# A GRU and an attention layer on one core: PSUM banks of two gates laid out by step instead of by sequence

## The reference

```python
def cell(h, x):
    gi = x @ W_ih + b_ih
    gh = h @ W_hh + b_hh
    i_r, i_z, i_n = jnp.split(gi, 3, axis=-1)
    h_r, h_z, h_n = jnp.split(gh, 3, axis=-1)
    r = jax.nn.sigmoid(i_r + h_r)
    z = jax.nn.sigmoid(i_z + h_z)
    n = jnp.tanh(i_n + r * h_n)
    h_new = (1.0 - z) * n + z * h
    return (h_new, h_new)
```

## Time and profile before

| | us |
|---|---|
| median of 3 runs | 746.58 (746.04 to 747.35) |
| the profiled execution | 746.35 |
| its span, first to last instruction | 744.5 |
| TensorE busy | 711.3 (96%) |
| VectorE busy | 580.8 (78%) |
| ACT busy | 484.9 (65%) |
| granted clock, mean | 0.996 |

### The profile page before, as it was taken

How to read it: one execution, slowest core, us unless ns; L and a number is a source line. 1 busy time by engine, 2 the same in 40 slices (tenths; PEclk the granted TensorE clock), 3 DMA queues, 4 the chain that set the end, 5 groups by cost and what they waited for, 6 DMA issues and landing times.

```text
span 744.5 us, 25735 instructions
## 1 busy us (share of the span) xinstructions
PE 711.3 (96%) x10644; PEld 525.3 (71%) x10644; DVE 580.8 (78%) x1625; ACT 484.9 (65%) x1665; POOL 104.4 (14%) x134
## 2 busy tenths in 40 slices
PE   6789999999999989999999999999999999999997
PEld 5688888888888767767667677676666767644555
DVE  5778888888888877777788888788887888834643
ACT  4455666556555666767787777776778776675453
POOL 0232222322322200000000101010110101000040
PEclk9999999999999999999999999999999999999999
DMA  6311121111211012222322222222232233300001
GB/s 237 100 48 46 47 83 51 46 45 46 88 38 40 3 30 43 44 37 49 46 44 44 43 45 44 43 44 49 40 50 43 45 52 37 47 19 29 29 6 52
DMA packets 77869, 36.74 MB, mean 49 GB/s; under 512 B 70540, under 2 KB 73784, under 8 KB 77752
## 3 DMA queue, kind: packets, MB, share of 16 engines
q1 hardware_dynamic: 77175, 33.52, 20.4%
q10 hardware_dynamic: 576, 1.57, 0.6%
HBM read 16.20 MB, written 2.10 MB: 25 GB/s over the span
## 4 chain that ended last, share of the span: by engine, by line
PE 83%; DVE 6%; ACT 4%; DMA 3%; issue 2%; SPq 1%; POOL 0%; DVEq 0%; POOLq 0%
PE bank L429 21%; PE bank L431 20%; PE bank L430 20%; PE bank L536 12%; PE bank L544 5%; DVE h_hi L1211 3%; DMA pT_lo<-p_lo 3%; PE bank L449 2%; ACT zg L937 2%; DVE nu L1205 1%; SPq L308 1%; PE bank L436 1%; DMA x<-in_x 1%; PE bank L458 0%; PE bank L478 0%
## 5 line engine op out<-in xcount | busy, mean ns | idle before, releaser
L431 PE MATMUL bank<-y_lo,w_hi 128*128 128x512 f16 (+2 forms) x496 | 139.8, 300 | 0.0
L429 PE MATMUL bank<-y_hi,w_hi 128*128 128x512 f16 (+2 forms) x496 | 139.7, 300 | 0.1
L430 PE MATMUL bank<-y_hi,w_lo 128*128 128x512 f16 (+2 forms) x496 | 139.8, 300 | 0.0
L536 PE MATMUL bank<-h_hi,whh_hi 128*128 128x16 f16 x1536 | 111.1, 177 | 17.6 <-DVE h_hi L1211 15.2
L536 PEld LDWEIGHTS bank<-h_hi,whh_hi 128*128 128x128 f16 x1536 | 88.8, 96 | 36.7 <-DVE h_hi L1211 34.1
L536 PE MATMUL bank<-h_hi,whh_lo 128*128 128x16 f16 x1536 | 109.5, 176 | 0.4 <-issue 0.4
L997 ACT ACTIVATE prob<-bank,nmx 128x128 f32<-128x128 f32 x256 | 90.4, 366 | 29.8 <-DVE nmx L1286 29.8
L536 PEld LDWEIGHTS bank<-h_hi,whh_lo 128*128 128x128 f16 x1536 | 89.4, 96 | 0.6 <-issue 0.5
L429 PE MATMUL bank<-w_hi,y_hi 128*128 128x128 f16 x512 | 89.1, 219 | 0.5 <-DVE v_lo L1290 0.5
L431 PE MATMUL bank<-w_lo,y_hi 128*128 128x128 f16 x512 | 89.1, 219 | 0.0
L430 PE MATMUL bank<-w_hi,y_lo 128*128 128x128 f16 x512 | 89.1, 219 | 0.0
(11 more groups left out here) (156 smaller groups left out, 2132.9 us busy)
## 6 DMA issues: line engine op xcount, KB each, us to landing
stage<-in_weights SPq DMA_DIRECT2D x16, 640.0 KB, 4.1
x<-in_x SPq DMA_DIRECT2D x16, 128.0 KB, 4.0
out<-xr SPq DMA_DIRECT2D x3, 512.0 KB, 3.1
xr<-in_ada_r SPq DMA_DIRECT2D x1, 1024.0 KB, 7.4
pT_hi<-p_hi SPq DMA_TRANSPOSE x64, 2.4
pT_lo<-p_lo SPq DMA_TRANSPOSE x64, 2.5
xr<-in_W_ih ACTq DMA_DIRECT2D x2, 384.0 KB, 3.9
xr<-in_W_hh ACTq DMA_DIRECT2D x2, 384.0 KB, 5.2
```

The source lines that it names most:

```text
L429: mm(ps, w[0], a[0], start=start, stop=False, skip_group_check=True)
L430: mm(ps, w[1], a[0], start=False, stop=False, skip_group_check=True)
L431: return mm(ps, w[0], a[1], start=False, stop=stop, skip_group_check=True)
L536: nc.tensor.matmul(out(m0 + m), half[:, k, (m0 + m) * P:(m0 + m + 1) * P], h_hi[:, k * B:(k + 1) * B, 1], start=False, stop=False, skip_gr ...
```

## The change

The banks of r and z are laid out by step: the word of `j` and `t` lies at `32 * t + j`. One step's 32 words are adjacent. The input products of m = 0 to 3 write in the order (step, sequence), 16 adjacent words for each step, and read their moving operand in that order as well. The operand stays where it was, so two words that are read one after the other lie 8 fp16 words (16 bytes) apart. `x_bias` writes 32 words of `pick`, eight times over, for r and z. The banks of n, their products and all counts of instructions stay.

```diff
-        r_cols, z_cols = ([ps[:, 0:BS * GB].rearrange("p (j t) -> p j t", t=BS) for ps in pair]
+        r_cols, z_cols = ([ps[:, 0:BS * GB].rearrange("p (t j) -> p t j", t=BS) for ps in pair]
...
-                for ps, at, width in ((r_bank, 0, GB), (z_bank, GB, GB), (n_bank, 2 * GB, 2 * GB)):
-                    nc.tensor.matmul(ps[n % 2][:, 0:BS * width], gpair[:, :],
-                                     pick[:, at:at + width].unsqueeze(2).broadcast_to([GK, width, BS]), start=True,
+                for ps, at in ((r_bank, 0), (z_bank, GB)):
+                    nc.tensor.matmul(ps[n % 2][:, 0:BS * GB], gpair[:, :],
+                                     pick[:, at:at + GB].unsqueeze(1).broadcast_to([GK, BS, GB]), start=True,
                                      stop=False, skip_group_check=True)
+                nc.tensor.matmul(n_bank[n % 2][:, :], gpair[:, :],
+                                 pick[:, 2 * GB:4 * GB].unsqueeze(2).broadcast_to([GK, 2 * GB, BS]), start=True,
+                                 stop=False, skip_group_check=True)
...
-                return (r_cols[n % 2][:, c, :], z_cols[n % 2][:, c, :], n_cols[n % 2][:, c, 1, :])[m // 2]
+                return (r_cols[n % 2][:, :, c], z_cols[n % 2][:, :, c], n_cols[n % 2][:, c, 1, :])[m // 2]
...
-                    nc.tensor.matmul(gate_cols(n, m), w[:, k, m * P:(m + 1) * P], a[:, n % 2, k, :], start=False,
+                    moving = a[:, n % 2, k, :]
+                    if m < 4:
+                        moving = moving.rearrange("p (b t) -> p t b", b=B)
+                    nc.tensor.matmul(gate_cols(n, m), w[:, k, m * P:(m + 1) * P], moving, start=False,
                                      stop=False, skip_group_check=True)
...
-                    return (r_cols[r % 2][:, c, s], z_cols[r % 2][:, c, s], n_cols[r % 2][:, c, 0, s])[m // 2]
+                    return (r_cols[r % 2][:, s, c], z_cols[r % 2][:, s, c], n_cols[r % 2][:, c, 0, s])[m // 2]
...
-                    nc.scalar.activation(zr[:, :, 1], r_cols[r % 2][:, :, s], ACT.Sigmoid).then_inc(r_ok, 1)
+                    nc.scalar.activation(zr[:, :, 1], r_cols[r % 2][:, s, :], ACT.Sigmoid).then_inc(r_ok, 1)
```

More of the change, by code:

```diff
@@ L934, in _ @@
                     act.wait_ge(r_mm, t1)
-                    nc.scalar.activation(zr[:, :, 1], r_cols[r % 2][:, :, s], ACT.Sigmoid).then_inc(r_ok, 1)
+                    nc.scalar.activation(zr[:, :, 1], r_cols[r % 2][:, s, :], ACT.Sigmoid).then_inc(r_ok, 1)
                     act.wait_ge(z_mm, t1)
-                    nc.scalar.activation(zg[:, :], z_cols[r % 2][:, :, s], ACT.Sigmoid).then_inc(z_ok, 1)
-                    nc.scalar.activation(zz[:, :, 1], z_cols[r % 2][:, :, s], ACT.Sigmoid, scale=-1.0)
+                    nc.scalar.activation(zg[:, :], z_cols[r % 2][:, s, :], ACT.Sigmoid).then_inc(z_ok, 1)
+                    nc.scalar.activation(zz[:, :, 1], z_cols[r % 2][:, s, :], ACT.Sigmoid, scale=-1.0)
                     act.wait_ge(npre_ok, t1)
```

## The result

The changed kernel takes 820.0 us (median of 4 runs, 818.2 to 820.3) against 746.8 us for the kernel before. The ratio is 1.0976, interval 1.0957 to 1.0995. The direction was forecast. The size was not: 73 us more instead of 11.8, beyond the range and beyond the dearer rival's 800 us.

A forecast was written before the change was run, and what follows sets the result against it. TensorE, nearly always busy, alternated in the recurrence with turns through ACT and VectorE; slower reads added 11.2 us in 13 blocks, 0.35 and 0.28 around blocks 0 and 1: 11.8 on 746.35, 758.2 us, range 745 to 792.

The forecast's parts named there:

- the dearer rival: Input products of m = 0 to 3 cost VectorE's far-read price, 177 to 229 ns each: 781 to 800 us; 24 in 100.
- The read's price: Input products of m = 0 to 3 on TensorE, read 16 bytes apart: 0.111 us each instead of 0.056.
- the prediction's own signs of being wrong: Cadence staying at 0.055 us or exceeding 0.15, first products' 0.105 us growing, or plain steps changing their 1.91 us.
- the smallest whole step above free: One extra access per word in the distant read, twice the old cadence: 0.111 us a product.
- The upper end: Price from VectorE's `rows_sum`, 256-byte steps: 1.38 to 1.79 ns a word, 177 to 229 ns a product.
- Rooms, counts and shares: Slow products behind s = 1 to 4: 7, 2, 13, 2; room for them: none, 0.21, 0.26, 0.09 us.
- a rule with two halves: Each access crossing to a new 16-byte line pays, yet 8 two-byte words may be strode over for free.
- The start-up: First 36 input products before the first step, already 0.105 us each: nothing charged; 2.5 us if 24 doubled.
- The writes: Input products of m = 0 to 3 writing rows of 16 adjacent words: nothing charged, as n products' runs of 8.
- ACT's reads and `x_bias`: Adjacent gate reads and bias matmuls: gain taken as 0, at most 0.3 and 0.8 us in all.
- The faster rival: Free read, and z products' last writes arrive 0 to 25 ns earlier each step: 744 us; 8 in 100.
- What makes up for it: Nothing after a late step recovers the time; the attention stage shifts whole, its length unchanged.

The follow-up runs named there:

- four adjacent products: Kernel before, with each input product of m = 0 to 3 issued four times, every one reading and writing adjacent words: 799.4 us.
- experiments 1: Kernel before with its old banks; only the moving operand of the products of m = 0 to 3 is read 16 bytes apart: 812.8 us, ratio 1.088.
- 3: Changed kernel's banks, with xb_hi and xb_lo laid out by step so every input product reads adjacent words; n products write 64 bytes apart: 747.7 us, ratio 1.0011.
- after: The changed kernel itself, against the kernel before: 820.0 us, ratio 1.0976.
- 2: Changed kernel's banks, but products of m = 0 to 3 read adjacent words and write each word 128 bytes from the last: 763.2 us, ratio 1.0217.
- spread: Changed kernel with its input products reordered, two slow then one fast, and shared evenly over the steps: 801.2 us.
- the candidate: New banks against the kernel before, a second load of x ordered by step for the conversions, and new shares of input products: 751.0 us, ratio 1.0095.
- experiment 5: Kernel before with its old banks and adjacent reads; products of m = 0 to 3 write each word 8 bytes from the last: 759.1 us.

## Why the prediction was wrong

**The read's price: the step that failed.** Two of the prediction's own signs of being wrong came: the cadence passed 0.15 us, and the first products' 0.105 us grew. The prediction took 0.111 us a product, "the smallest whole step above free", between 0.056 and 0.229. Measured: 0.226. The upper end had been read from VectorE's sum over states, 1.79 ns a word in the form of 160 words, and set aside because its stride is 256 bytes. The runs show 1.77 ns a word on TensorE at 16 bytes and 1.80 at 32, so distance beyond 16 bytes was no reason to discount it. That TensorE pays what VectorE pays may be chance: VectorE's form of 96 words has 1.38 ns a word, and no run here varies VectorE's reads. With 0.229 us the prediction's own sum gave 800 us; the run with four adjacent products, which has that length without the slow reads, took 799.4, of which its start-up is 2 us dearer than the slow reads'. Rooms, counts and shares were right: 7 products behind s = 1 cost 15.5 us in 13 blocks where 13 x 7 x 0.171 is 15.6, and those behind s = 3 cost 26.2, where 13 x (13 x 0.171 - 0.26) is 25.5.

The Trainium skill, SBUF — State Buffer, section "Door 1: The DMA port swizzle", was cited for a rule with two halves. Its lines of 16 bytes agree with the runs (half the price at 8 bytes, no more at 32 than at 16). Its remark that 8 two-byte words may be strode over for free does not: that is the distance that cost four times as much, and 4 words cost twice. Free here were 2.

**The clock: missing from the prediction.** No rival had it. It is worth some 21 us of the 73: with reads priced right the forecast would have been 800 and still 20 us short. Four fifths of it sit in steps that the price of the reads hardly touches (s = 2 with two slow products, s = 4 likewise). The trace of before could have warned: its start-up runs at 0.105 us a product, and from 42.5 to 45.9 us, in block 2, the granted clock is 0.50. So the level does change within the recurrence, and the change was going to hold TensorE for 5 us of each block on words that arrive at a quarter of the rate. Why the clock falls is shown only so far: with distant reads it falls, with adjacent work of the same length it does not.

**The start-up.** I charged nothing, since 0.87 ns a word would have met the 0.82 already there. At 0.226 us a product it is 24 x 0.12 = 2.9 us; the first step starts 3.1 us later.

**The writes.** The price of rows of 16 words, 0, holds (experiments 1 and 3). The reason given, that the n products' runs of 8 words are free, holds as well, but says nothing on single words, which cost double.

**ACT's reads and `x_bias`.** Right: 198 ns for `zg` against 197, and no change in the three bias matmuls beyond the clock.

**The faster rival.** Its mechanism is there and small: the last six steps take 11.48 to 11.49 us in all five traces with the new banks (after, 2, 3, spread and the candidate) and 11.51 to 11.52 in all with the old. In these steps `zg` starts 206 ns behind the start of the last z product instead of 213, so it is the tail that shrank; 7 ns is what 16 columns take at 0.43 ns, the extra that a strided write costs by experiment 5. Of this the step keeps 0.004 to 0.005 us, 0.6 us over 128, a third of the 0.015 from which it would decide. The Trainium skill, PSUM — Partial Sum Buffer, section "Specifications (TRN2)", says any non-contiguous pattern slows matmuls significantly. For single words apart the runs agree (0.11 against 0.056 us); for runs of 8 words they do not (0.056 us); and for 16 columns the cadence of 0.024 us does not show it, only the 7 ns of the tail do.

**What makes up for it.** Nothing does, as forecast: the stage behind the recurrence takes 487.7 us before and 488.9 after.

## What to carry to other kernels

A layout that makes one engine's access adjacent makes another's strided; price the strided side by the number of lines that it touches, and look for any row in the trace that reads so, on whichever engine, before discounting it. The product that is paced by its operand does not only last longer. Here it also let the granted clock fall, and then work that was not changed, and was hidden, comes onto the path. To tell the two apart, replace the starved instruction by several unstarved instructions of the same total length.

## What the runs showed of the hardware

- TensorE reads a moving operand of two-byte words in about 1.8 ns for each line of 16 bytes newly touched (128 words in 0.114 us at 8 bytes, 0.226 at 16, 0.230 at 32), at granted 0.50 and 1.00 alike (thirteen products in 2.96 and 2.97 us); up to 4 bytes between words this is hidden (0.058 us).
- TensorE writes a word that is not adjacent to the last in about twice its column time (0.11 us for 128 words at granted 1.00, 0.21 at 0.50), at 8, 64 and 128 bytes alike.
- Behind groups of reads at 16 or 32 bytes the granted clock falls to 0.50 although the busy rows show no gap (mean over the recurrence 0.78 in the changed kernel). Adjacent work of the same length leaves it at 1.00, and so do reads at 8 bytes, at 0.114 us a product. The mean over the recurrence hides this, since the level is only ever one of two.
